# Cross-attention block on one Trainium2 core: GELU of six and two MLP units at two steps, with the MLP pieces of the matrix engine laid out anew around both

## The reference

```python
h = _layernorm(x, ln1_g, ln1_b)
x = x + _mha(h, h, sa_wq, ...)                 # self attention: 2048 keys
h = _layernorm(x, ln2_g, ln2_b)
x = x + _mha(h, context, ca_wq, ...)           # cross attention: 1601 keys
h = _layernorm(x, ln3_g, ln3_b)
h = jax.nn.gelu(h @ mlp_w1.T + mlp_b1, approximate=False) @ mlp_w2.T + mlp_b2
return x + h                                   # mlp: 256 -> 1024 -> 256
```

## Time and profile before

| | us |
|---|---|
| median of 3 runs (lowest, highest) | 1604.9 (1602.36, 1605.7) |
| the profiled execution | 1600.0 |
| its span, first to last instruction | 1598.3 |
| PE matmul busy | 1470.2 (92%) |
| ACT busy | 1068.1 (67%) |
| DVE busy | 536.6 (34%) |
| mean granted PE clock, share of full | 0.963 |

### The profile page before, as it was taken

How to read it: one execution, slowest core, us unless ns; L and a number is a source line. 1 busy time by engine, 2 the same in 40 slices (tenths; PEclk the granted TensorE clock), 3 DMA queues, 4 the chain that set the end, 5 groups by cost and what they waited for, 6 DMA issues and landing times.

```text
span 1598.3 us, 21199 instructions
## 1 busy us (share of the span) xinstructions
PE 1470.2 (92%) x8062; PEld 636.2 (40%) x8062; DVE 536.6 (34%) x1286; ACT 1068.1 (67%) x1285; POOL 44.0 (3%) x62
## 2 busy tenths in 40 slices
PE   8889999998874999999999999699999999999967
PEld 5567777776331222322322322232223432432334
DVE  2445555556541022231330431233232133143140
ACT  2323333332433999999999999589788787797831
POOL 2100000000110000000000000000000000000000
PEclk9999999999896999999999999799899999999988
DMA  7300000000496000010010254501000000000000
GB/s 237 145 7 8 6 7 7 7 3 0 97 249 112 11 21 11 11 39 21 11 37 20 31 84 85 112 21 47 12 21 11 25 11 11 21 15 1 7 7 14
DMA packets 37672, 64.07 MB, mean 40 GB/s; under 512 B 6164, under 2 KB 21844, under 8 KB 37428
## 3 DMA queue, kind: packets, MB, share of 16 engines
q1 hardware_dynamic: 32024, 40.87, 12.3%
q0 software_dynamic: 5552, 21.89, 3.8%
HBM read 40.85 MB, written 22.02 MB: 39 GB/s over the span
## 4 chain that ended last, share of the span: by engine, by line
PE 71%; ACT 17%; DVE 4%; DMA 4%; issue 3%; SPq 0%; DVEq 0%; ACTq 0%; POOL 0%; POOLq 0%
PE PS L954 22%; PE PS L937 15%; ACT PX L677 14%; PE PS L756 6%; PE PS L765 6%; PE PS L1011 5%; PE PS L1023 4%; PE PS L994 2%; PE PS L802 2%; DMA k_parts<-KPARTS 2%; PE PS L728 1%; PE PS L774 1%; PE PS L777 1%; PE PS L973 1%; PE PS L732 1%
## 5 line engine op out<-in xcount | busy, mean ns | idle before, releaser
L677 ACT ACTIVATE PX<-PS 128x1024 f32<-128x1024 f32 (+1 forms) x928 | 883.6, 1040 | 163.5 <-PE PS L937 114.3
L954 PE MATMUL PS<-PX,V 128*32 128x512 f32 (+1 forms) x3712 | 499.4, 610 | 5.0 <-ACT PX L677 3.0
L937 PE MATMUL PS<-QST,stack 50*128 50x512 f32 (+1 forms) x1856 | 385.3, 472 | 44.0 <-DMA stack<-k_parts 22.7
L937 PEld LDWEIGHTS PS<-QST,stack 50*128 50x128 f32 (+1 forms) x1856 | 155.8, 185 | 445.2 <-ACT PX L677 342.6
L954 PEld LDWEIGHTS PS<-PX,V 128*32 128x32 f32 (+1 forms) x3712 | 73.7, 108 | 152.1 <-issue 126.3
L1373 DVE COPY OT<-PS 128x512 f32<-128x512 f32 x32 | 22.1, 692 | 313.0 <-PE PS L954 311.7
L604 ACT ACTIVATE PR<-PS,small 128x1601 f32<-128x1601 f32 x16 | 25.6, 1597 | 106.8 <-DVE small L1210 106.8
L756 PE MATMUL PS<-tokF,XT 128*128 128x512 f32 (+1 forms) x256 | 95.0, 525 | 0.6 <-DVE small L1142 0.6
L765 PE MATMUL PS<-tokT,PT 128*128 128x256 f32 (+1 forms) x416 | 93.3, 381 | 0.6 <-DVE CZ L1259 0.6
L765 PEld LDWEIGHTS PS<-tokT,PT 128*128 128x128 f32 (+1 forms) x416 | 77.9, 190 | 10.7 <-issue 0.8
L1023 PE MATMUL PS<-W,HIDT 128*128 128x256 f32 x256 | 65.2, 404 | 10.6 <-ACT HIDT L663 9.8
(11 more groups left out here) (134 smaller groups left out, 1148.6 us busy)
## 6 DMA issues: line engine op xcount, KB each, us to landing
QST<-q_parts SPq DMA_DIRECT2D x192, 64.0 KB
q_parts<-PARTS POOLq DMA_DIRECT2D x16, 512.0 KB, 5.4
stack<-k_parts SPq DMA_DIRECT2D x24, 256.0 KB, 9.7
stack<-k_parts SPq DMA_DIRECT2D x24, 200.1 KB, 7.1
k_parts<-KPARTS POOLq DMA_DIRECT2D x8, 512.0 KB, 12.2
v_cross<-V POOLq DMA_DIRECT2D x1, 3328.0 KB, 10.0
V<-v_cross SPq DMA_DIRECT2D x2, 1664.0 KB, 13.8
k_parts<-PARTS POOLq DMA_DIRECT2D x6, 512.0 KB, 3.4
```

The costliest lines, as they stand in the source:

```text
L677: act.activation(PX[0:kr, (2 * t + half) % 4, :, :], PS[0:kr, slot:slot + 2, :], ACT.Exp, scale=SCALE).then_inc(at["exp"], 1)
L937: ins = pe.matmul(PS[0:kr, 2 * (n % LOOK) + jj, :], KST[a][lo:lo + NROW, pair, kt * P:kt * P + kr].bitcast(F32R), QST[lo:lo + NROW, pair, ...
L954: ins = pe.matmul(PS[32 * j:32 * j + 32, 6, :], V[0:kr, kt, 2 * (g // 2 * GH + j) + g % 2, :], PX[0:kr, (2 * t + j // 2) % 4, j % 2, :], s ...
```

## The change

The GELU is split in two: units 0 to 5 after the exponentials of step 31, units 6 and 7 after those of step 36. The m and o pieces are at other steps. Unit 4 is whole at step 27 (it was at 29 and 30), unit 5 at 29 and 30, unit 6 whole at 32, unit 7 at 33 and 34 (it was whole at 35). The first output tile has its three parts of units 0 to 5 at step 37 and the fourth at 38; the tiles behind it follow at 39/40, 43/45 and 46/48. A part of tile 0 waits for the first GELU if it takes unit 0, and for the second if it takes unit 6.

```diff
-    {"y": [5, 7, 9, 11], "h": [17, 18], "m": list(range(19, 27)) + list(range(29, 35)) + [35, 35],
-     "o": [37, 37, 39, 39, 42, 42, 43, 43, 45, 45, 46, 46, 48, 48, 49, 49]},
+    {"y": [5, 7, 9, 11], "h": [17, 18], "m": list(range(19, 27)) + [27, 27, 29, 30, 32, 32, 33, 34],
+     "o": [37, 37, 37, 38, 39, 39, 40, 40, 43, 43, 45, 45, 46, 46, 48, 48]},
...
-GELU_STEP = 36
+GELU_STEPS = ((31, 0, 6), (36, 6, 8))
...
-            def gelu(q):
-
-                act.wait_ge(at["unit_taken"], HID // P * (q + 1))
-                act.activation(HIDT[:], HIDT[:], ACT.Gelu).then_inc(at["gelu"], 1)
+            def gelu(q, lo, hi):
+
+                act.wait_ge(at["unit_taken"], HID // P * q + hi)
+                act.activation(HIDT[:, lo:hi, :], HIDT[:, lo:hi, :], ACT.Gelu).then_inc(at["gelu"], 1)
...
-                    if a == 1 and t == GELU_STEP and not first:
-                        gelu(c - 1)
+                    if a == 1 and not first:
+                        for step, lo, hi in GELU_STEPS:
+                            if t == step:
+                                gelu(c - 1, lo, hi)
...
-                    elif first:
-                        pe.wait_ge(at["gelu"], q + 1)
+                    else:
+                        for n, (_, lo, _) in enumerate(GELU_STEPS):
+                            if i == 0 and lo in share(HID // P):
+                                pe.wait_ge(at["gelu"], len(GELU_STEPS) * q + n + 1)
```

## The result

| | us |
|---|---|
| before, median of 7 runs (lowest, highest) | 1604.9 (1602.32, 1608.89) |
| changed, median of 7 runs (lowest, highest) | 1614.9 (1609.07, 1622.4) |
| ratio of the changed kernel to the one before, 95% interval | 1.0062 (1.0038 to 1.0086) |
| profiled execution, before and changed | 1600.0 and 1622.4 |

The changed kernel is slower, by 10 us of median, 6 to 14 by the interval. The forecast was slower by 4.6, 1609.5 with a range up to 1612.5. The direction held, the size was half of what came. The profiled execution is the slowest of the seven, so it can't be set against the one of before as a whole: of its 22.4 us, 6.1 lie ahead of cross attention, 1.4 in the first cross chunk and 2.5 in the tail, where the two programs do the same work in the same order. Chunks 1 to 3 hold 12.5. What follows goes by chunks and steps.

The account below looks back on a forecast made before the run. Steps without a piece were taken as bound by ACT, steps with pieces by PE. Step lengths gave +2.2 and two clock falls +2.4, so 1604.9 + 4.6 = 1609.5, range 1604.5 to 1612.5.

Parts of the forecast that it names:

- both hidden groups: Unit 6's pair under the first GELU pause and tile 0's first three parts under the second, each at cost 0.
- the first GELU not held by DVE: Before the first GELU, DVE takes unit 5 at 1343.5, exponentials end at 1344.2: no wait, 0.6 of room.
- The term of step 28: Unit 4's two m parts at step 27 plus a wait make step 28 longer by 2.43 us, near 4.3.
- The wait: At step 27 PE stands 0.50 us until DVE has taken unit 3 and bank 7 is free.
- the stop in the first pause: PE stands idle 2.5 us while ACT is away at the first GELU, after unit 6's pair.
- the 2.2 of the sum: All step-length terms over three chunks, +0.74 per chunk, before any cost of the clock.
- the clock behind the first pause: After the first GELU pause the granted clock falls to 0.50 in two of three chunks, 1.2 each: +2.4 us.
- my two ends: Price of one clock fall behind the first pause: low end 0.46, high end 1.7 (half of a 3.42 low stretch).
- The clock holds: Rival: the clock falls behind none or one of the first pauses, +2.2 to +3.4, 1607.1 to 1608.3; chance 0.30.
- PE the bound throughout: Rival: only PE's own stops count, gain 1.62 per chunk, 4.9 in all, 1600.0; chance 0.10.
- A drain with each switch: Rival: the added table switches on ACT take 2.75 us more per chunk, 8.3 in all, 1617.8; chance 0.03.
- Parts not hidden: Rival: step 37's three parts run behind the second pause, 2.9 us per chunk, 8.7 in all, 1618; chance 0.05.

Follow-up runs that it names:

- e5: e1 with one more added part at step 32, three in all, same result, so no stop of PE is left in the first pause: 1607.4, ratio 1.0007.
- e8: The changed kernel once more, without any edit, for a second profiled execution: 1617.1, ratio 1.0065.
- e3: The changed kernel with the last output tile at steps 48 and 49 instead of 46 and 48: 1614.6, ratio 1.0057.
- e10: The changed kernel with the scores of half-steps 0 and 2 of chunks 1 to 3 computed twice, same result: 1616.0, ratio 1.0068.
- e1: The changed kernel with the two parts of unit 6 at step 32 computed twice, as useless work under the first pause: 1615.1, ratio 1.0049.
- e4: The kernel before, one GELU at step 36, with only the output tiles moved to steps 37/38, 39/40, 43/45 and 46/48: 1606.8, ratio 1.0001.
- e2: The changed kernel with unit 7 also whole at step 32, so four m parts lie under the first pause: 1604.7, ratio 0.9997.
- e7: e2 with both parts of unit 3 at step 25 and none at 26: 1601.5, ratio 0.9977.
- e6: The steps of the changed kernel with the one GELU of all units at step 36, no split: 1610.6, ratio 1.0035.
- e9: e7 with the scores of half-steps 0 and 2 of chunks 1 to 3 computed twice, same result: 1600.1, ratio 0.9974.

## Why the prediction was wrong in size

**Right: what bounds the kernel, and the lengths of steps.** The reading that ACT bounds free steps and PE the steps with pieces gave +0.74 per chunk from the step lengths. Measured without a fall (e5): 0.68 and 0.64. The pieces of it hold too: step 31 lasts 7.82 (forecast 7.8), step 36 5.62 (5.6), the GELUs and loads as above, both hidden groups hidden, the first GELU not held by DVE. The term of step 28 was 0.2 too high (4.05 against 1.83 + 2.43). The wait was 0.40 and not 0.50, and two m parts back to back take 1.91 us, not twice 1.06; the pair at step 35 of the kernel before shows it (start of its m matmuls to start of the next scores):

```profile
1352.54 1.98 PE L1011 MATMUL PS<-HC,W 128*128 128x512 f32 x4
...
1354.45 0.74 PE L937 MATMUL PS<-QST,stack 50*128 50x512 f32 x4
```

The same slip made the stop in the first pause 2.5 in the forecast for 2.73. In three chunks all this makes 2.0 for the 2.2 of the sum.

**Right in kind, wrong in count and size: the clock behind the first pause.** The forecast was two falls in three pauses at 1.2 each, 2.4. In every kernel that kept the stop of 2.7 us (changed, e8, e3, e10) the clock fell in every chunk, twelve of twelve. Over the two traces of the changed kernel steps 33 and 34 exceed the 4.51 of e5 by 1.5, 1.6, 2.5 and 1.6, 2.5, 1.6, on average 1.9; three make 5.7. The step that failed in the count was to rank the new stop by its length between stops of 1.7 and 3.3 us: e1 shows that 1.0 us was enough at this place. That what follows the pause on PE (two score matmuls and a stop of 0.4) takes part in it is likely, and no run tests it by itself. The price failed on its upper end: I took half of one low stretch of 3.4 us, but the stretch may go on, 6.8 us in one chunk of each of the two traces. Where it lasted 3.4 the price was 1.5 to 1.6, inside my two ends; where it lasted 6.8 it was 2.5, outside. Taken from these traces, the term makes 3.3 of the 5.4 us that the forecast lacked against the median.

**Missing: the chunk starts.** The sum had no term for a fall anywhere but behind the pause. Both traces of the changed kernel have falls at the starts of chunks 2 and 3, with steps 0 to 3 at 10.30 and 11.84 and then 11.82 and 10.28 against 8.95: 4.2 us in each. The trace of before has none, so nothing there gave the term away. With these, 2.0 + 5.7 + 4.2 = 11.9 of the 12.5 us by which chunks 1 to 3 of the profiled execution are longer; the rest is a low stretch at the start of chunk 1 that both kernels have and that reached further into it here (steps 0 to 3 last 12.17 against 11.47). In the median 2.0 + 5.7 leaves 2.3 of the 10 us. That the chunk starts are these 2.3 fits, and is not shown.

**What stays open.** How often the falls at chunk starts come in runs without a profile, and whether the change makes them likelier. Where the last tile stands doesn't decide it (e3, e4). They were seen in seven of the ten starts of chunks 2 and 3 of changed, e8, e3, e2 and e7, in none of the ten of before, e4, e6, e1 and e5, and in none of the four with doubled scores. Part of this is likely chance of the execution, since e1 and e5 have the steps of the changed kernel around the chunk's start and no fall there. A place that all kernels share shows that falls come and go without a change: in the first cross chunk all twelve traces have a stop of PE of 1.3 us, until DVE has copied OT. The clock fell there in two of them, the changed kernel's and e5's. In the changed kernel:

```profile
1086.98 1.71 PE L956 MATMUL PS<-PX,V 128*32 128x512 f32 x8 [1.31 <-DVE OT L1377]
```

The pv behind this stop took 1.7 us for 1.07. So the length of a stop alone does not tell whether the clock falls: 1.3 us did it in two of twelve there, 1.0 us in three of three in e1.

**The rivals.** The clock holds: no; it fell behind the first pause in every chunk. In e5, where it held, the median is 2.0 above that of before. PE the bound throughout: no; it asks for chunks that are 1.62 us shorter where the clock holds, chunks 2 and 3 of e5 are 0.68 and 0.64 longer, and free steps stay at 1.82. A drain with each switch: no; the loads follow in 0.01 to 0.02 us. The Trainium skill's figure for a switch (ScalarE: Activation LUTs, What ACT_TABLE_LOAD costs), about 2.66 us, was not what these six more switches cost. Parts not hidden: no; all twelve matmuls are done before the exponential behind the second pause lets the next scores go.

## What to carry over

A pause of one engine is not free cover. Work moved under it saves its own time, but what is left of the stop can be paid again when the matrix engine comes back at the low clock. Here this took 5.7 us, as much as hiding the pair of unit 6 was reckoned to save (3 x 1.93). So fill the pause until no stop is left, if need be by moving one more unit into it, and look at what the engine does right behind it. Where a doubt remains whether a low clock is a cause, add work that changes nothing: a kernel that gets faster by doing more has told it.

## What the runs showed of the hardware

- At the first pause, the granted clock went to 0.50 around or behind the end of a stop of TensorE of 2.7 us in 12 of 12 pauses, behind 1.0 us (with 0.4 close behind) in 3 of 3 (e1), and in none of 3 with 0.15 and 0.42 (e5). It also held in 9 of 9 pauses of e2, e7 and e9, where 0.9 us of idle lay between two blocks of m matmuls, and 0.3 at most behind the last. I had expected that shorter stops than those of before would often pass.
- A stop of 1.3 us in the first cross chunk, the same in all twelve traces, was followed by a fall in two.
- Behind the first pause most low stretches lasted 3.4 us, some went on for 6.8, one of e10 for 10.2, although PE was busy in them nearly all the time (6.35 of 6.83 in e8, 10.09 of 10.24 in e10).
- At the starts of chunks 2 and 3 the clock fell with no stop over 0.7 us, in seven of 24 starts.
- Table loads of 1.28 us follow the last exponential in 0.01 to 0.02 us. GELU takes 1.06, 2.76 and 3.62 us for 1024, 3072 and 4096 elements per partition.
